# The last four tiles of the state-space loop three units apart instead of four, the last output blocks begun two units earlier, and four edits in the routing chain behind the loop

## The reference, cut to what matters

```
h   = x @ W_base^T + b_base + 2 * LoRA mixture(cond_8[b])
for direction in (forward, reversed):              # a Mamba block
    xs, z = split(h @ in_proj^T); xs = silu(conv4(xs)); dt = softplus(...); B, C from xs
    h_t = exp(dt*A) * h_(t-1) + dt*xs*B            # scan over the tokens, 16 states n
    y   = (sum over n of C_n*h_n + D*xs) * silu(z)
x   = x + out_proj(y_forward + y_reversed)
X   = x @ w_bot[b]^T + bias                        # w_bot: 8 masked weights mixed by cond_8
out = x + X + sum over the top 2 of 8 experts e of
      W2[e]^T( silu(W1[e] xs_) * (W3[e] xs_) ),    xs_ = X * softmax weight of that expert
```

## Time and profile before

| | before |
|---|---|
| median of 3 runs | 1400.84 us (1396.48 to 1401.32) |
| profiled execution: its own time | 1394.14 us |
| its span, first to last instruction | 1392.3 us |
| PE busy | 1294.3 us (93%) |
| DVE busy | 940.7 us (68%) |
| POOL busy | 964.5 us (69%) |
| mean granted clock of TensorE, share of full speed | 0.978 |

### The profile page before, as it was taken

The page is one execution under the profiler, slowest core; times in us unless marked ns, Lnnn a source line. Parts: engine busy times, 40 slices in busy tenths (PEclk is TensorE's granted clock), DMA queues, the critical chain, the costliest instruction groups (busy, mean ns, idle before and its releaser), DMA issues. The chain is left out here.

```text
span 1392.3 us, 16616 instructions
## 1 busy us (share of the span) xinstructions
PE 1294.3 (93%) x5296; PEld 778.4 (56%) x5296; DVE 940.7 (68%) x1140; ACT 723.1 (52%) x1296; POOL 964.5 (69%) x511
## 2 busy tenths in 40 slices
PE   8999989999999989899797878899999999999997
PEld 3443333344333333333343333457999999999996
DVE  3999999999999999999999999963111111111110
ACT  4888776778785677676767564413111111111111
POOL 1999999999999999999999999832222222222211
PEclk9999999999999999999999999999999999999999
DMA  5555465555556464555456554508988888888982
GB/s 209 181 167 176 160 166 166 166 167 173 173 171 181 149 184 153 165 168 176 159 181 186 185 174 146 189 8 310 351 312 315 319 316 324 301 323 316 324 306 46
DMA packets 105497, 290.40 MB, mean 209 GB/s; under 512 B 9649, under 2 KB 19506, under 8 KB 89922
## 3 DMA queue, kind: packets, MB, share of 16 engines
q1 hardware_dynamic: 95762, 271.24, 56.3%
q0 software_dynamic: 9648, 18.09, 6.5%
HBM read 271.47 MB, written 9.96 MB: 202 GB/s over the span
## 5 line engine op out<-in xcount | busy, mean ns | idle before, releaser
L451 PE MATMUL ps_y<-arena,ident 128*128 128x512 f32 x1020 | 497.3, 619 | 55.0 <-POOL arena L1204 54.7
L1204 POOL TENSOR_TENSOR arena<-arena 128x1024 f32<-128x1024 f32 x192 | 457.4, 2404 | 18.9 <-DVE arena L946 15.3
L451 PEld LDWEIGHTS ps_y<-arena,ident 128*128 128x128 f32 x1020 | 190.9, 195 | 322.9 <-issue 214.0
L1188 POOL TENSOR_TENSOR arena<-arena 128x1024 f32<-128x1024 f32 x127 | 303.9, 2393 | 6.0 <-issue 4.3
L737 ACT ACTIVATE ps_de<-arena,An 128x512 f32<-128x512 f32 x256 | 176.2, 688 | 225.2 <-DVE arena L943 224.3
L1257 POOL DMA_INDIRECT out_x<-arena x39 | 61.8, 1584 | 319.1 <-ACT arena L881 301.9
L927 DVE TENSOR_TENSOR ps_u<-ps_du,arena 128x512 f32<-128x512 f32 x256 | 178.6, 698 | 23.9 <-DVE arena L957 8.6
L1155 DVE TENSOR_TENSOR arena<-ps_du,arena 128x512 f32<-128x512 f32 x39 | 27.0, 691 | 232.8 <-PE ps_du L617 232.8
L737 ACT ACTIVATE arena<-arena,An 128x512 f32<-128x512 f32 x256 | 181.0, 707 | 0.0
L943 DVE TENSOR_TENSOR_SCAN arena<-ps_de,hlast,arena 128x512 f32<-128x512 f32 x128 | 163.0, 1274 | 1.0 <-ACT arena L737 1.0
L943 DVE TENSOR_TENSOR_SCAN arena<-ps_de,arena 128x512 f32<-128x512 f32 x128 | 155.3, 1214 | 3.7 <-ACT arena L737 3.7
(11 more groups left out here) (225 smaller groups left out, 1484.2 us busy)
## 6 DMA issues: line engine op xcount, KB each, us to landing
arena<-bc_scratch SPq DMA_DIRECT2D x256, 512.0 KB, 4.6
arena<-in_W SPq DMA_DIRECT2D x117, 1024.0 KB, 8.2
arena<-arena POOLq DMA_DIRECT2D x15, 512.0 KB, 5.0
arena<-in_xT SPq DMA_DIRECT2D x2, 1024.0 KB, 6.1
arena<-in_w2c SPq DMA_DIRECT2D x1, 2048.0 KB, 8.6
arena<-in_xT SPq DMA_DIRECT2D x4, 512.0 KB, 6.1
X_scratch<-stg SPq DMA_DIRECT2D x12, 128.0 KB, 4.8
out_x<-stg SPq DMA_DIRECT2D x12, 128.0 KB, 5.1
```

Source lines behind the costliest of these rows:

```text
L451: t = e.matmul(Y[j][:, :], ident[:, :], hc[:, i % NP, j, :], start=False, stop=(n == 15))
L1188: e.tensor_tensor(uA[:, turn % 2, :, :], duA.rearrange("p (o t) -> p o t", o=1).to_broadcast([128, 2, TH]), ring[:, turn % NR, 0, :, :], A ...
L1204: e.tensor_tensor(hc[:, i % NP, :, :], hh[:, i % NH, :, :], c, ALU.mult).then_inc(gp_hc, 1)
```

## The change

1. The four tiles of the second half of sequence 1 move from the units 46, 50, 54 and 58 of pass 3 to 46, 49, 52 and 55. Their transposes, logits, copies and stores follow, since all are placed relative to the tile.
2. The first parts of the last two output blocks move from iteration NU-2 (block 0) and NU (block 1) to NU-4 and NU-2, units 60 and 62 of pass 3.
3. `xT2` begins with the channel block 0 once output block 0 is ready, and waits for block 1 only after that.
4. `warm(2, 2)` is removed, and `warm(6, 5)` becomes `warm(3, 5)`.
5. `lx` gets a place of its own, and the waits of `hidden` on its stores go.
6. POOL's four additions (and with them SP's four stores of their results) move behind the first three fetches, and on SP behind the weight loads of tile 1.

```diff
-           at(3, 46): (1, 4), at(3, 50): (1, 5), at(3, 54): (1, 6), at(3, 58): (1, 7)}
+           at(3, 46): (1, 4), at(3, 49): (1, 5), at(3, 52): (1, 6), at(3, 55): (1, 7)}
...
-        lx = hT.rearrange("p a k t -> p (a k t)").rearrange("p (i c) -> p i c", i=4)
...
+        lx = af.view(4, 2 * C)
...
-                if i == NU - 2:
-                    out_block(1, 0, 0, side, (0, 1))
+                if i in (NU - 4, NU - 2):
+                    out_block(1, 0, (i - NU + 4) // 2, side, (0, 1))
...
-                if i == NU:
-                    out_block(1, 0, 1, both_side, (0, 1))
...
-            for k in range(2):
-                is_free(("o", 1, 0, k))
             for h2 in range(2):
-                for c in range(2):
-                    p = place["xT2", h2, c][0]
-                    for k in range(2):
+                for k in range(2):
+                    is_free(("o", 1, 0, k))
+                    for c in range(2):
+                        p = place["xT2", h2, c][0]
                         t = e.matmul(PS[p][:, 0:C], wbot[:, 1, k, c * 128:c * 128 + 128],
                                      X[1][:, k, h2 * C:h2 * C + C], start=(k == 0), stop=(k == 1))
-                    t.then_inc(full[p], 1)
+                        if k == 1:
+                            t.then_inc(full[p], 1)
...
-            warm(2, 2)
...
-            warm(6, 5)
+            warm(3, 5)
...
-                elif c == 0:
-                    for k in (2 * i, 2 * i + 1):
-                        e.wait_ge(l_lx[k], 16)
-                        e.wait_ge(l_st[2 + k], 16)
...
             for i in range(3):
                 fetch(i)
+            for i in range(4):
+                is_read(e, ("x2", 1, i))
+                x2, xt = lx[:, i, 0:C], lx[:, i, C:2 * C]
+                e.tensor_tensor(xt, xt, x2, ALU.add).then_inc(gp_sB, 1)
             for k in range(4):
                 e.wait_ge(l_st[2 + k], 16)
...
             load_2(0, at_0)
+            e.wait_ge(l_xi[0], 16)
+            load_13(1, at_1)
+            load_2(1, at_1)
             for i in range(4):
                 e.wait_ge(gp_sB, i + 1)
                 e.dma_start(out[T + i * 128:T + i * 128 + 128, :], lx[:, i, C:2 * C]).then_inc(l_st[2 + i], 16)
-            e.wait_ge(l_xi[0], 16)
-            load_13(1, at_1)
-            load_2(1, at_1)
             load_13(2, at_2)
```

More of the change, by code:

```diff
@@ L1237, in _ @@
             e.tensor_copy(eid[:, :], cmpt[:, :, 1]).then_inc(gp_ei, 1)
[L1238 to L1241, removed]
             e.wait_ge(dv_rt, RT["tok"])
```

## The result

| | before | after |
|---|---|---|
| median of 15 runs each, taken together | 1398.14 us (1394.97 to 1401.6) | 1404.05 us (1401.51 to 1407.86) |
| ratio of the two | | 1.0037, 95% interval 1.0029 to 1.0046 |
| profiled execution, span | 1392.3 us | 1402.4 us |
| mean granted clock, share of full speed | 0.978 | 0.970 |

The change makes the kernel slower, by 5.9 us of the median, where the prediction had 0.7 us faster. That is 0.4%, less than the 0.5% that the prediction held to be indistinguishable from nothing, and yet clear of noise: the two sets of 15 runs barely touch, with 1401.6 us the highest before and 1401.51 the lowest after. The 1400.84 us of three runs, from which the prediction counted, lay 2.7 us above the median of all 15.

The account below looks back on a forecast made before the run. DVE was taken to set the pace in the loop, PE in the expert loop. Terms +1.7 - 0.4 - 2.0 = -0.7 us, carried to 1400.84 - 0.7 = 1400.1 us; range 1395 to 1405.

Parts of the forecast that it names:

- Unit 49: Pass 3: the tile issued between two additions makes DVE wait longer at L971, +1.7 us, bounds +0.7 and +2.2.
- The other tiles: Units 46 to 56: PE idles up to 2 us before each tile, but additions stay in time; costed at nothing.
- rival (b): Units 49 to 56: idle before tiles lowers the clock, PE falls behind, up to +4 us, 1404; chance 0.17.
- End of the loop: PE's last additions begin earlier without the output block's first part at iteration 64: -0.4 us, bounds 0 and -0.5.
- `xT2`: Behind the loop: two of eight matmuls need only block 0 and move ahead of DVE's second block: -0.9 us, certain.
- `warm(2, 2)`: Counting: without this filler last_x2 begins 2.2 us earlier, meets half clock for +1.0, and ends 1.2 us earlier.
- rival (c): Clock stays at 1.2 GHz over all of last_x2, up to 3.8 us more, about 1402.3 us; chance 0.13.
- By the page: Sentence on last_x2: at half clock all through, its 7.6 us would cost 3.8 more instead of 1.0.
- First tile: First expert tile starts 2.4 us earlier; the second's wait for weights leaves a gain of 1.3, in full 2.7.
- the sum of -2.0: Whole chain behind the loop, with the -0.9 and -1.2 in it: -2.0 us, bounds -1.3 and -2.7.
- `lx` and the stores: Own place of lx, dropped waits of hidden, later stores: nothing, with 1 to 2 us to spare at the fourth fetch.
- the wait that was named as a sign of being wrong: Expert loop: a wait of DVE for the fourth fetch, listed among the signs that would show the prediction wrong.

Follow-up runs that it names:

- best1: best0 plus W1 of expert tile 1 issued early, as soon as the four last tiles are copied: 1396.11 us against 1398.19, ratio 1.0 (0.9985 to 1.0014).
- best3: best0 with warm(2, 5) behind the four last tiles replaced by warm(1, 5) directly ahead of them: 1402.59 us, ratio 1.0036.
- b_nofiller: The kernel before without warm(2, 2), nothing else: 1404.33 us, ratio 1.0042.
- a_tile50: The changed kernel, without filler, with the four tiles in units 46, 50, 53, 56: 1399.18 us, ratio 1.0014.
- best0: The kernel before with new xT2 order, warm(1, 2) in place of warm(2, 2), and the first-expert-tile edits: 1395.59 us against 1398.19, ratio 1.0.
- b_first_tile: The kernel before with only the first-expert-tile edits (warm(3, 5), place of lx, additions and stores moved): 1398.18 us against 1398.53, ratio 1.0003.
- b_tiles: The kernel before with only the four tiles moved to units 46, 49, 52, 55: 1400.59 us, ratio 1.0011.
- a_filler: The changed kernel with warm(2, 2) put back, nothing else: 1396.52 us against 1398.62, ratio 0.9991.
- a_mid: The changed kernel with warm(1, 5) between the first and second of the four last tiles: 1400.58 us, ratio 1.0023.
- a_narrow: The changed kernel with eight matmuls of 128 columns in the place of warm(2, 2): 1397.82 us, ratio 0.9999.
- a_filler1: The changed kernel with half the filler, warm(1, 2), put back: 1397.26 us, ratio 1.0002.
- a_nobias: The changed kernel, without filler, with the bias matmuls (L528) of the four last tiles left out: 1395.19 us, ratio 0.9980.

## Why the prediction was wrong, point by point

- **Unit 49**, +1.7: right. +1.8 in the profile after, +1.7 with the tiles alone, by the wait that was named.
- **The other tiles**, nothing: nearly right for the tiles of the change. PE stood idle 1.89 us ahead of the tile of unit 52, and in the profile after DVE did not wait. In four of seven profiles with these tiles the clock fell there and DVE waited 0.24 us, which is rival (b) in small. Not foreseen: 0.5 us less from unit 49 to the last product in the profile after, 0.15 in those four. Three 0.20 us pauses behind DVE's own products (the L927 that follow L957) became one, which fits the small work of the tiles now lying in units 51 and 59, where it covers them; that is read from two timelines and was not tested.
- **End of the loop**, -0.4: not shown. The stage was 2.30 us before and 2.17 after, but 2.02 and 2.14 in two other profiles with the old places.
- **`xT2`**, -0.9: right, 0.85.
- **`warm(2, 2)`: the step that failed.** "It will be `last_x2` that meets this: from 933.8 to 935.8 at half clock, +1.0." I took the end of the low clock in the trace of before, 935.8, as a point in time that the work behind it would meet. In the changed kernel nothing ended it there. The low clock lasted to 956, and cost 6.5 us on the tiles and 1.3 on the filler behind, where the sum had 1.0. The filler put back took this cost away (1396.52 us), and taken from the kernel before it brought it there (1404.33). The earlier trace rows had shown both, the filler and the return at its end; they did not show which was the cause. The prediction carried this only as "+0.5 if the clock stays low over `last_x2`" and as rival (c), both at half their price.
- **Rival (c)** was this very mechanism, at 0.13, and priced at half: 7.6 us of work, timed at full clock, take 7.6 us more at half clock, not 3.8. The same slip stands in the prediction's sentence "By the page". At its right price the rival comes to 1406.7, beyond the range of 1395 to 1405.
- **The median of 1404.05 inside that range is luck.** The top of the range was drawn from rival (b), tiles too close for PE, at 1404; that is not what happened.
- The advice of the Trainium skill, "TensorE: Matmul & The Clock Gate", section "Why this matters for your kernels", to keep dense work on TensorE, was weighed and set aside because the clock fell in spite of the filler. For this filler the measurements side with the page: its removal from the kernel before cost 0.42%. In most profiles with a filler the clock fell all the same, and was back soon; with the tiles alone moved it did not fall at all. Work without a pause was not enough, however: from 937.30 to 952.4 after the change PE had none, and the clock stayed at 1.2 GHz.
- **First tile**, in the sum of -2.0: of the two ends I had given, the lower came. Tile 1 waited 1.4 us for its weights. From the start of L591 to the end of the span, the profiles with these edits lie between 0.1 us below before and 1.0 above it, most within 0.15 (best1 and best3, which edit more there, left out). With the clock back (half the filler) the whole chain behind the loop gave 1.7 us, against 2.0.
- **`lx` and the stores**: nothing, right for the time, but the wait that was named as a sign of being wrong did appear. The fourth fetch waited for the stores until 982.04, and DVE then for the fetch (timeline of DVE):

```profile
988.68 0.35 DVE L1141 TENSOR_SCALAR arena<-arena 128x256 f32<-128x256 f32 x1 [2.97 <-DMA arena<-X_scratch,arena]
```

  DVE had nothing else to do there. PE needed these rows at 991.84 and did not wait, so some 2.8 us were to spare.

## What to carry to other kernels

A filler matmul has to be read for what the clock does after it, not for whether it prevented a fall; taking it out may cost a doubling of the work behind it, here of four tiles (8.37 us became 14.88). Before a low-clock stretch in a trace is taken as fixed, ask what ended it. When a time has two groups, compare the mean clock of single executions before trusting a median. A stage that differs in two timelines should be looked up in every other profile with the same code before it is explained. And moved work that shares banks in turn (tiles, output blocks) should be priced as one edit: alone, one of them blocked PE for 6 us.

## What the runs showed of the hardware that was not expected

- TensorE can be busy for 14 us without a pause and stay at 1.2 GHz (938 to 952 after the change, clock 0.50 in every row; the same 14.88 us from the last tiles to the filler in b_nofiller). It did so twice with one-row matmuls among its work. With these left out it was back at 942, but in a_tile50 it was back at 939 with them in place, so they are not shown to be the cause.
- The outcome varies between executions of one program: with half a filler (best0) 8 of 12 executions lay at 1392.7 to 1396.9 us, and 4 at 1402.6 to 1405.2. The fall behind the logits varies too: with all other things in that stretch as before, it lasted 3.4 us in the profiles before and b_first_tile and did not occur in b_tiles.
- Around idle times of 2.2 to 2.8 us the granted clock went to 1.2 GHz at three places (units 46 and 53 of pass 3, and L591 in best3, 13.91 us instead of 7.3). Ahead of the tile of unit 52 an idle time of 1.89 us was followed by 1.2 GHz in four profiles (b_tiles, a_filler, a_mid, a_narrow) and by full clock in three (after, a_filler1, a_nobias).
